# Expert layer of a decoder kernel: a low half before the weights' split, expert 0's bias tiles at its start, one drain on Pool

## The reference

```
probs = softmax(x @ Wr + br);  gate, idx = max, argmax      # one expert for each row
pos = position of the row in its expert's queue; rows beyond the capacity C = 512 are dropped
expert_in[e] = gate * x at its slot
h  = relu(expert_in[e] @ W1[e] + b1[e])
eo = h @ W2[e] + b2[e]
out = x + gate * eo of its slot
```

## Time and profile before

| | |
|---|---|
| median of 3 runs | 1347.86 us (1347.41 to 1349.51) |
| profiled execution | 1342.3 us, its span 1340.3 us |
| mean granted TensorE clock | 0.989 |
| TensorE busy | 1294.3 us, 97% of the span |
| VectorE busy | 946.4 us, 71% |
| ScalarE busy | 660.4 us, 49% |
| Pool busy | 402.0 us, 30% |
| the experts' part | from about 1130 us to the end |

### The profile page before, as it was taken

One profiled execution on the slowest core, in us unless ns is written; L12 is line 12 of the kernel. 1 busy time (PEld: TensorE's weight loads), 2 busy tenths in 40 slices (PEclk: granted clock), 3 DMA queues, 4 the chain that ended last, 5 costly groups with the idle time before them and its releaser, 6 DMA issues.

```text
span 1340.3 us, 31438 instructions
## 1 busy us (share of the span) xinstructions
PE 1294.3 (97%) x12285; PEld 1055.1 (79%) x12285; DVE 946.4 (71%) x1872; ACT 660.4 (49%) x1837; POOL 402.0 (30%) x476
## 2 busy tenths in 40 slices
PE   7999899999999999999999999999999998999997
PEld 7988677777777778888888888888888885778785
DVE  6549678888886776777777777777766875666662
ACT  4456333443333655555555554555555642555651
POOL 3213444554432111131122212221212232454342
PEclk9999999999999999999999999999999998999999
DMA  7962142222333111011021120210204015444520
GB/s 259 338 205 64 65 145 95 93 79 95 105 96 105 55 48 41 17 67 53 17 74 46 39 82 9 72 49 17 76 12 134 17 56 182 158 161 143 199 74 20
DMA packets 68656, 122.69 MB, mean 92 GB/s; under 512 B 12249, under 2 KB 20465, under 8 KB 68514
## 3 DMA queue, kind: packets, MB, share of 16 engines
q1 hardware_dynamic: 60194, 97.11, 21.8%
q0 software_dynamic: 8320, 23.62, 5.0%
HBM read 82.13 MB, written 42.07 MB: 93 GB/s over the span
## 4 chain that ended last, share of the span: by engine, by line
PE 81%; DVE 11%; ACT 5%; issue 2%; DMA 1%; POOL 1%; SPq 0%; DVEq 0%; ACTq 0%; POOLq 0%
PE bank L70 18%; PE bank L72 17%; PE bank L71 17%; PE bank L2161 6%; PE bank L2149 6%; PE bank L2182 4%; PE bank L2174 2%; PE bank L2269 2%; PE bank L1262 1%; PE bank L1232 1%; PE bank L2657 1%; ACT b_prob L1549 1%; PE bank L1206 1%; PE bank L2233 1%; PE bank L2222 1%
## 5 line engine op out<-in xcount | busy, mean ns | idle before, releaser
L1549 ACT ACTIVATE b_prob<-bank,b_neg_top 128x155 f32<-128x155 f32 x496 | 187.3, 407 | 117.9 <-DVE b_neg_top L1741 117.9
L70 PE MATMUL bank<-turned_h,big_h 128*128 128x512 f32 x320 | 131.2, 410 | 1.8 <-DVE turned_l L1936 1.5
L72 PE MATMUL bank<-turned_h,big_l 128*128 128x512 f32 x320 | 126.2, 394 | 0.0
L71 PE MATMUL bank<-turned_l,big_h 128*128 128x512 f32 x320 | 125.5, 392 | 0.0
L1741 DVE TENSOR_REDUCE b_neg_top<-bank 128x6 f32<-128x930 f32 (+1 forms) x93 | 94.3, 1014 | 28.5 <-PE bank L2161 28.3
L70 PE MATMUL bank<-b_wo_h,b_ot_h 128*128 128x512 f32 x256 | 113.2, 442 | 0.4 <-DVE b_ot_l L1770 0.4
L2149 PEld LDWEIGHTS bank<-ident,b_prob 128*128 128x128 f32 x640 | 93.4, 191 | 24.7 <-DVE b_pt L1758 8.6
L2149 PE MATMUL bank<-ident,b_prob 128*128 128x128 f32 x640 | 103.5, 284 | 5.6 <-DVE b_pt L1758 4.8
L1549 ACT ACTIVATION_READ_ACCUMULATOR b_prob<-bank,b_neg_top 128x1 f32 x496 | 102.6, 207 | 0.0
L72 PE MATMUL bank<-b_wo_h,b_ot_l 128*128 128x512 f32 x256 | 101.6, 397 | 0.0
L1752 DVE TENSOR_TENSOR b_prob<-b_prob,b_recip 128x930 f32<-128x930 f32 (+1 forms) x93 | 98.5, 1059 | 3.4 <-DVE b_recip L1749 0.2
(11 more groups left out here) (315 smaller groups left out, 3370.9 us busy)
## 6 DMA issues: line engine op xcount, KB each, us to landing
wide<-in_L_ffn_W_dram SPq DMA_DIRECT2D x16, 1024.0 KB, 5.5
slot_rows<-empty_row SPq DMA_DIRECT2D x8, 1032.0 KB, 13.4
a_xr<-in_x_dram SPq DMA_DIRECT2D x32, 256.0 KB, 2.7
x_scratch<-a_xr SPq DMA_DIRECT2D x32, 256.0 KB, 2.3
tiles<-x_scratch SPq DMA_DIRECT2D x32, 256.0 KB, 3.4
rows<-x_scratch SPq DMA_DIRECT2D x32, 256.0 KB, 3.5
out_dram<-rows SPq DMA_DIRECT2D x32, 256.0 KB, 2.0
rows<-slot_rows SPq DMA_DIRECT2D x7, 1032.0 KB, 8.0
```

The lines of the kernel that those rows point to most:

```text
L70: pe.matmul(out, lh, rh, start=first, stop=False)
L71: pe.matmul(out, lh, rl, start=False, stop=False)
L72: return pe.matmul(out, ll, rh, start=False, stop=last)
L1549: last = act.activation(prob[:, n % 2, j, h:h + 2 * L2 - 1:2], s_banks[:, h, o:o + L2], ACT.Exp, bias=neg_top[:, n % 2, h, j:j + 1], accum ...
```

## The change

Three edits, all in `experts`:

- VectorE: `h_low(e, 3)` moves before `weights(e + 1, 1 - par, 0)`; `tail(e + 1, 1 - par)` moves from before the four `finish` to behind them, ahead of the second weights' split.
- ScalarE: the four `first_bias` leave the chunk loop of expert 0 and stand in `prepare(0, 0)`, before its first ReLU, behind a `hold` on the load of expert 0's biases.
- Pool: in the expert without a next one (expert 7) a `drain()` is issued before the waits and scatters.

No operation other than the drain and that `hold` is added, and none is removed.

```diff
@@ pool @@
         def work(e, par, more):
             if more:
                 prepare(e + 1, 1 - par)
+            else:
+
+                pool.drain()
             for k in range(G):
                 hold(pool, s["res_made"], G * e + k + 1)
@@ act @@
         def prepare(e, par):
-            pass
+
+            hold(act, s[f"b_loaded{par}"], 32)
+            for k in range(G):
+                first_bias(k)
...
                 act.activation(ht_h[:, c, :], h[:, c % 2, :], ACT.Copy).then_inc(s["h_high"], 1)
-                if isinstance(e, int) and e == 0:
-                    first_bias(c)
                 if c == 1 and more:
                     weights(e + 1, 1 - par, 0)
@@ dve @@
             h_low(e, 2)
+            h_low(e, 3)
             if more:
                 weights(e + 1, 1 - par, 0)
-            h_low(e, 3)
-            if more:
-                tail(e + 1, 1 - par)
             for k in range(G):
                 finish(e, par, k)
...
             if more:
+                tail(e + 1, 1 - par)
                 weights(e + 1, 1 - par, 1)
```

## The result

The changed kernel takes 1337.54 us (median of 6 runs, 1336.42 to 1339.34) against 1347.63 for the kernel before (6 runs, 1344.86 to 1349.51): a ratio of 0.9929, with a 95% interval of 0.9914 to 0.9943. The profiled execution took 1337.9 us, its span 1336.1.

A forecast was written before the change was run, and what follows sets the result against it. TensorE, busy 97% of the span, was taken as the bound, with time to win only where it stands still or runs slowly; 2.10 + 1.62 + 2.07 = 5.79 us off 1347.86 gave 1342.1 us, range 1339.0 to 1345.6.

The forecast's parts named there:

- The sum without the drain: Whole kernel: 2.10 and 1.62 us in expert 0 plus 2.07 in experts 1 to 6, 5.79 us less.
- the drain's: Pool in expert 7: the new drain hides in 12.08 us of idle, cost 0, gain at most 0.84 us.
- Expert 0's chunk 3: Expert 0, second layer: TensorE resumes 2.56 us after the last first-layer matmul's start, not 4.66, a gain of 2.10 us.
- The clock's 1.62 us: Expert 0 behind TensorE's stop: seven matmuls take 2.37 us at full clock, not 3.99; bounds 0 and 1.62.
- Rival 2: Expert 0: the clock falls anyway, gain only 4.17 us, 1343.7 us; chance 0.06.
- Pool against the split: Loop's experts: VectorE's weights' split comes 0.1 us before Pool's addition, which waits; cost 0.
- Rival 1: Loop's experts: Pool comes first at the splits, the 2.07 us are lost, 1344.1 us; chance 0.10.
- Rivals 3 and 4: Whole kernel: no change in timed runs, about 1346.5 us, chance 0.11; slower by waits for Pool, 1359.8, chance 0.06.
- The tail: VectorE, behind the last finish: two small operations on 4 columns delay only the second weights' split, needed half an expert later.
- The third turn's cover: Expert 2, second layer: the next expert's first low half is done 0.9 us before TensorE asks for it, no cost.
- The later load of W1: SyncE's queue: the W1 load of two experts ahead is issued some 2.4 us later, with some 10 us of cover.
- The profiled execution: Whole kernel: 1342.3 us before, 1336.5 forecast; the runs' median stays 5.6 us above it.

The follow-up runs named there:

- e2: The changed kernel without the new drain in expert 7: 1342.61 us against 1348.33 for the kernel before, ratio 0.9962.
- e1: The kernel before with the drain in expert 7 as its one edit: 1343.57 us against 1348.33, ratio 0.9971.
- e3: The kernel before with only VectorE's new order (low half before the split, tail last): 1343.65 us against 1348.33, ratio 0.9964.
- e4: The kernel before with only expert 0's four bias tiles moved to its start: 1344.98 us against 1348.33, ratio 0.9976.
- e5: The changed kernel with the tail back between the first weights' split and the first finish: 1340.50 us, before 1349.24, ratio 0.9929.
- e6: The changed kernel with the drain moved from expert 7 to the start of the experts' part on Pool: 1341.12 us, before 1349.24, ratio 0.9932.
- e7: The changed kernel with a second drain at the start of the experts' part on Pool: one execution, 1341.76 us, before 1349.24.
- e10: The kernel before, unchanged, profiled again: one execution, 1346.27 us, beside 1339.76 for the same kernel.
- e9: The changed kernel with the drain moved into expert 6, ahead of Pool's additions for expert 7: one execution, 1333.97 us, before 1339.76.
- e12: The changed kernel with TensorE's wait for the low half moved to the third matmul, which reads it: 1334.85 us, before 1347.69, ratio 0.9899.

## Why the prediction was wrong, point by point

- **The sum without the drain was right.** It said 5.79 us, made of 2.10 + 1.62 in expert 0 and 2.07 in experts 1 to 6. The traces show 3.71 and 2.03, and e2, which is this sum's kernel, 5.7 us by the medians, 5.1 by the ratio. The interval of 3.0 to 7.3 us can't tell the terms apart; that each is right is shown by the traces.
- **The step that failed is the drain's: "Its cost lies in that idle time: 0. Bounds: ... a gain of at most the 0.84 us between the end of a `finish` and its scatter's start".** The cost was indeed hidden. The gain was 4.6 us, as the drain takes over what the block's own drain does at the end, 4.97 us down to 0.38 (e1 alone: 4.8 us faster). The bound looked only at what lies between the new drain and the scatters, and not at what Pool does behind them. "No row shows a drain" was true of the rows shown, but the trace of before holds one of 4.97 us as its end, and even without it there was a hint: from the last scatter's start (1332.71) to the span's end it is 7.6 us, of which the landing takes 2.1. With this term the forecast would have been 1337.5; that it meets the measured 1337.54 so closely is luck, as the interval is 1.9 us to either side.
- **Expert 0's chunk 3** went as described, the distance 2.57 us against 2.56. That the bias tiles by themselves give 0.1 us beside the order is shown by e3; that Pool's additions lengthened the low half to 1.75 us by e4, where it takes 0.68.
- **The clock's 1.62 us** was taken in full. It was there in three of four traces with that gap, so a mean over executions would be about 1.2, an estimate from four traces. Rival 2, a low clock in spite of a short gap, appeared in no trace.
- **Pool against the split**: VectorE came first by 0.1 us in six experts and by 0.3 in expert 3, the split took 2.28 and the addition 3.1 to 3.3. Rival 1 did not occur, and no run makes Pool come first at a split.
- **Rivals 3 and 4** (no change in the timed runs; slower) did not occur either: the ratio's interval, 0.9914 to 0.9943, excludes both, and the third turn began without a wait.
- **The tail** was costed at nothing for being late, which was right, but its move was not an idle one: left in place it would have eaten the loop's 2.07 us in the trace (e5). The forecast saw that Pool gets its turn after the split and asked what would stand there in the new order, but not what the tail would have cost at its old place.
- **The third turn's cover** was 0.9 us by the forecast and is 1.1. The later load of W1 made nobody wait.
- **The profiled execution** was forecast at 1336.5 and took 1337.9, which is luck: the experts' part gained 11.9 us and not 5.8, and the stages in front took 7.7 us more than in the trace of before. The runs' median lay 5.3 us above the profiled execution before and 0.4 below it after; that this distance stays was a bad assumption, on which the forecast of the median, 1347.86 - 5.79, does not hang. The range's lower bound, 1342.1 less 0.84 and 2, is 1339.2 and not 1339.0; the measured time lies below either.
- **Not in the forecast and not of the change**: expert 0's first layer takes 11.0 or 12.6 us (13.1 and 13.7 in e6 and e7). Each of the two values occurs with the bias tiles between the chunks (before 12.6, the same kernel in e10 11.0) and ahead of them (e2 12.6, changed 11.0). The difference is the clock at its start, as the first 3.6 us show (in e6 and e7 the granted clock is 0.50 there, and still 0.87 and 0.70 in the next 3.6 us), in the window of before

```profile
1130.70:1134.30 3.60, 3.59 (x9) 2.78 (x10) 0.01 (x1) 0.00 (x0) 0.00 (x0) 0.56 1.07 405
```

and in that of the changed kernel (9 matmuls at a granted clock of 0.56, 16 at 1.00):

```profile
1138.40:1142.00 3.60, 3.58 (x16) 2.96 (x17) 0.02 (x1) 2.13 (x4) 3.60 (x3) 1.00 1.06 399
```

This chance accounts for 1.6 of the 12 us by which the two traces differ; without it they would differ by 10.3, as the medians do by 10.1.

## What to carry to other kernels

Bound an added instruction by what it can take away from a later one of its kind, and read the end of the trace down to the last instruction of every engine: 5 us stood there that no busy time showed. When a queue is reordered, ask for each operation that can be made to wait by another engine what it will stand beside afterwards; here, in the traces, the place of a copy of four columns was worth as much as the edit that was meant. And compare two traces from a common point on, since the untouched stages in front moved by up to 10 us from execution to execution.

## What the runs showed of the hardware

- A drain on Pool takes about 0.08 us for each scatter issued since the last drain (0.38, 0.71, 2.67 and 4.97 us for 4, 8, 32 and 60), and nothing for additions between. Placed where Pool idles it cost nothing, and the last one was short (e1, e2). The drains at the start of the experts' part in e6 and e7 and the moved one of e9 took longer, and why stays open.
- A VectorE operation with two SBUF operands and a Pool addition exclude each other for the length of one whole operation, in the order in which they come: the addition took 3.33 us and not 1.29 behind a split that began 0.1 us earlier, VectorE's low half 1.75 and not 0.69 behind an addition. A copy of 128x4 in float32 waits likewise (1.26 us in e5, 0.16 in the changed kernel). The Trainium skill, "GPSIMD Engine Reference", section "8. Key points", names, as instructions of VectorE that contend with Pool, those in a two-port mode beside those with two SBUF inputs; in which mode the copy ran, no row shows. An operation on PSUM and one SBUF operand didn't wait (0.75 us in the middle of Pool's additions).
- After the same idle of 2.16 us TensorE kept 2.4 GHz in one execution and fell to 1.2 GHz in three; after 0.47 us or less it kept 2.4 GHz in every trace.
- A stop of TensorE of 0.23 us cost 0.33: the start behind the matmul that waited came 0.34 us later, where 0.23 is usual (e12 against the changed kernel).
